# Moving the rotary update behind the fold and the normalisation in VectorE's order of a decoder's multi-query attention

## The reference

```
q = (x @ Wq + bq) in 16 heads;  k = x @ Wk + bk;  v = x @ Wv + bv
q, k = apply_rope(q), apply_rope(k)        # the first 4 of each head's 8 features are turned
att = softmax(causal(q @ k^T / sqrt(8)))
out = (att @ v in all heads) @ Wo + bo
x   = layernorm(x + out)
```

## Time and profile before

| what | value |
|---|---|
| three executions | 2307.48, 2312.87, 2314.32 us (median 2312.87) |
| the profiled execution's own time | 2307.48 us |
| its span | 2305.7 us |
| PE busy over the span | 1649.5 us (72%) |
| DVE busy | 1348.5 us (58%) |
| ACT busy | 915.9 us (40%) |
| POOL busy | 575.1 us (25%) |
| the stage of the change | from about 1548 to 1706 us of the span |
| length of one of its steps in the steady part | 9.12 to 9.21 us |

### The profile page before, as it was taken

How to read it: one execution, slowest core, us unless ns; L and a number is a source line. 1 busy time by engine, 2 the same in 40 slices (tenths; PEclk the granted TensorE clock), 3 DMA queues, 4 the chain that set the end, 5 groups by cost and what they waited for, 6 DMA issues and landing times.

```text
span 2305.7 us, 45150 instructions
## 1 busy us (share of the span) xinstructions
PE 1649.5 (72%) x14699; PEld 1055.1 (46%) x14699; DVE 1348.5 (58%) x4103; ACT 915.9 (40%) x2551; POOL 575.1 (25%) x965
## 2 busy tenths in 40 slices
PE   4443499477765565579777852138979999996998
PEld 3332355344433353445444521125547777774443
DVE  2333556466667756631675666756756666663776
ACT  2222444367531123224343433223336566563343
POOL 2321422111112222210122223431214434442010
PEclk9999999599977777789898975559999999997999
DMA  5000000000000000000002000000000000000000
GB/s 197 1 1 1 1 1 0 1 1 0 0 1 0 0 0 0 0 0 1 1 0 95 0 1 0 0 0 1 0 1 1 1 0 0 0 1 1 0 0 18
DMA packets 2926, 18.86 MB, mean 8 GB/s; under 512 B 1049, under 2 KB 1177, under 8 KB 1561
## 3 DMA queue, kind: packets, MB, share of 16 engines
q1 hardware_dynamic: 2842, 17.76, 2.1%
HBM read 16.64 MB, written 1.05 MB: 8 GB/s over the span
## 4 chain that ended last, share of the span: by engine, by line
PE 51%; issue 26%; DVE 7%; ACT 5%; POOL 5%; POOLq 4%; DVEq 2%; DMA 0%; ACTq 0%; SPq 0%
PE ps L2685 5%; PE ps L901 3%; PE ps L915 3%; PE ps L2250 3%; PE ps L2260 3%; PE ps L2274 3%; POOL arena L345 3%; PE ps L2229 3%; PE ps L2236 2%; PE ps L970 2%; PE ps L1438 2%; PE ps L2094 2%; PE ps L327 2%; PE ps L535 2%; PE ps L880 2%
## 5 line engine op out<-in xcount | busy, mean ns | idle before, releaser
L345 POOL TENSOR_TENSOR arena<-arena,C 128x1 f32<-128x1 f32 (+1 forms) x272 | 155.7, 574 | 810.8 <-DVE arena L356 499.0
L1060 DVE TENSOR_REDUCE arena<-ps 128x4 f32<-128x512 f32 x256 | 164.1, 686 | 90.1 <-PE ps L911 50.0
L2187 POOL TENSOR_TENSOR arena<-arena 128x512 f32<-128x512 f32 x128 | 132.7, 1042 | 234.3 <-DVE arena L2475 233.8
L436 POOL TENSOR_TENSOR arena<-arena,C 128x512 f32<-128x512 f32 x96 | 99.8, 1040 | 365.1 <-ACT arena L637 126.7
L1028 ACT ACTIVATE arena<-ps 128x512 f32<-128x512 f32 x256 | 132.2, 604 | 90.0 <-PE ps L927 90.0
L1438 PE MATMUL ps<-hid,WA 128*20 128x16 f32 x1024 | 57.3, 197 | 108.4 <-DVE hid L1481 108.4
L2685 PE MATMUL ps<-WA,arena 128*128 128x512 f32 x256 | 133.7, 604 | 0.4 <-ACT arena L2709 0.4
L2384 ACT ACTIVATE arena<-ps,arena 128x256 f32<-128x256 f32 x256 | 119.9, 478 | 11.9 <-issue 8.1
L2393 ACT COPY arena<-ps 128x512 f32<-128x512 f32 x128 | 69.1, 589 | 121.7 <-PE ps L2260 121.7
L1895 PE MATMUL ps<-C,arena 128*128 128x128 f32 x32 | 14.3, 469 | 133.2 <-ACT arena L1943 92.2
L2467 DVE TENSOR_REDUCE arena<-ps 128x2 f32<-128x512 f32 x128 | 82.5, 687 | 43.9 <-PE ps L2250 42.5
(11 more groups left out here) (412 smaller groups left out, 4204.6 us busy)
## 6 DMA issues: line engine op xcount, KB each, us to landing
WA<-w_late SPq DMA_DIRECT2D x1, 4228.0 KB, 13.6
R<-rows SPq DMA_DIRECT2D x1, 1858.0 KB, 8.4
WA<-w_early SPq DMA_DIRECT2D x1, 1600.0 KB
WB<-w_rest SPq DMA_DIRECT2D x1, 1152.0 KB, 12.9
xT_all<-x_T SPq DMA_DIRECT2D x1, 1024.0 KB, 6.8
x_all<-x_tok SPq DMA_DIRECT2D x1, 1024.0 KB, 15.2
arena<-mask SPq DMA_DIRECT2D x1, 1024.0 KB
ctxT_all<-ctx_T SPq DMA_DIRECT2D x1, 1024.0 KB
```

Of the source, the lines that this page charges most:

```text
L345: nc.gpsimd.tensor_tensor(v_(s, cols, "rstd", 0, n), v_(s, cols, "mv", 1, 2 * n - 1)[:, ::2] if n > 1 else v_(s, cols, "mv", 1, 1), cst("m ...
L436: return eng.tensor_tensor(heads(v_(s, ATT, dst, of, 512)), v_(s, ATT, src).unsqueeze(1).broadcast_to([128, 4, 128]), cst("tilemask").unsq ...
L1060: red = nc.vector.tensor_reduce(v_(z, ATT, "m", 4 * t, 4), heads(ps[z][t][:, :]), AXX, ALU.max)
L2187: nc.gpsimd.tensor_tensor(p, p, v_(z, LAT, "rec", 4 * u + 2 * x, 2).unsqueeze(2).broadcast_to([128, 2, 256]), ALU.mult).then_inc(l_sub, 1)
```

## The change

In VectorE's order of one step of `S_MQA`, the three instructions of `rope` for the next sequence move from ahead of the wait for `mT_ps` to behind the fold operand (line 1110) and `normed`, and stay ahead of `added`. Nothing is added or removed, and no other engine's order is touched.

```diff
@@ satt_dve, step @@
                 cut_up(s)
                 if before:
                     divided(i, s)
-                if sub == S_MQA and after:
-                    rope(i, s, 1)
                 dve.wait_ge(mT_ps, nth(st, i, s))
                 nc.vector.tensor_tensor(heads(v_(s, ATT, "P", FOLD, 256).bitcast(BF16)),
                                         ps[(s + 1) % 2][2][:, 0:128].unsqueeze(1).broadcast_to([128, 4, 128]),
@@
                                         ALU.mult).then_inc(m_fold, 1)
                 if before and not (isinstance(i, int) and 2 * i + s < 2):
                     normed(i, s, -2)
+                if sub == S_MQA and after:
+                    rope(i, s, 1)
                 if before:
                     added(i, s)
                 if after:
```

## The result

The changed kernel took 2342.31 us (median of four executions, 2341.67 to 2342.97), against 2313.35 us before (2307.48 to 2314.32). The ratio is 1.0129, with a 95% interval of 1.0113 to 1.0145: 29.0 us slower by the medians. The prediction was 2334 us with a range up to 2341, so the direction held and the size was above the range.

A forecast was written before the change was run, and what follows sets the result against it. PE was taken to bound the stage, its scores coming to wait for POOL's spreading. The 22.7 us sum gave 2330.2 us on the profiled time or 2335.6 on the median; predicted 2334 us, range 2326 to 2341.

The forecast's parts named there:

- The fold operand gained nothing: On DVE, L1110 waits for PE's L950, not the moved work, so it starts as before except in the first step.
- the slack of the spreading: Before the scores (L901), POOL's L436 had 0.87 us of usable slack; the rotary update moves 2.43 us later.
- `y_read` costs nothing further: L1086 starts at 1617.12 instead of 1616.46, but its `y_read` still comes before L436 ends at 1618.32.
- the sum: Delay of the scores (L901) over 15 steps: 19.8 + 1.3 + 1.6 = 22.7 us, with none made up.
- The clock.: In the changed stage, PE 79% busy with one 1.7 us gap per step was expected to keep clock 1.00.
- this rival: Granted clock falls in the changed stage: some 2460 us, or 2395 us if half the steps are hit; chance 3%.
- rows 1 and 9: Evidence against a fall: 1120 to 1220 us busy 75% at clock 0.99; LSTM stage busy 47% at 1.00.
- the 1.09 us from the start of L436 to that of L901: Term from POOL's spreading to PE's scores, taken from the first step, within the 3.29 us from L1110 to L901.

The follow-up runs named there:

- both repairs of PE's order: Changed kernel with seven extra matmuls per step in PE's gap and the wait for POOL's spreading last of the three before the scores: 2333.77 us.
- the gap filled with matmuls: Changed kernel with seven extra unread matmuls per step on PE between the fold and the scores: 2333.83 us.
- spreading twice: Kernel before, with POOL's spreading done twice in each step of the changed stage, VectorE's order untouched: 2318.58 us.
- only the sum moved: Against the kernel before, only the rotary update's sum moved behind the fold operand and `normed`, its two products staying ahead of the wait: 2323.77 us.
- the other order: Changed kernel with the rotary update directly behind the fold operand and the normalisation behind it: 2338.44 us.
- order of the waits: Changed kernel with the wait for POOL's spreading put last of the three in front of the scores, in the changed stage alone: 2338.45 us.
- spreading three times: Kernel before, with POOL's spreading done three times in each step of the changed stage, VectorE's order untouched: 2342.36 us.

## Why the prediction was right or wrong, step by step

**Right: the mechanism.** The fold operand gained nothing, the slack of the spreading was used up, the scores wait for POOL, `y_read` costs nothing further, and nothing behind the scores made the delay up. The size of the chain can be checked without the two effects that the sum lacked: with both repairs of PE's order the stage takes 157.95 us scores to scores against 134.99 before, 22.96 us more, where the sum said 22.7. By the medians of these two kernels it is 20.2 us.

**Wrong, the larger part: "The clock."** The prediction held the granted clock at 1.00, gave its fall 3% and had nothing for it in the sum. It fell in five steps, and the gap filled with matmuls shows what that cost: 167.61 - 159.92 = 7.7 us in the stage, 8.5 us by the medians. At the gap of 1.7 us that the prediction forecast itself it falls too. Neither row that was set against the fall carries the argument.

The earlier trace rows give the LSTM stage a clock of 1.00. The same stage of the kernel with the gap filled, which no edit touches, has 0.50 in that row, with matmuls of the same length: 194 ns in the median for L1438 (there L1443) and 388 ns for L1420 (there L1425). And behind that stage, in the kernel before, the same two matmuls take 0.73 us at 273.73 and 0.39 us at 288.49, while the clock row says 1.00 all the way. First the window of the kernel with the gap filled, then rows of the kernel before:

```profile
40.00:230.00 190.00, 88.71 (x1317) 60.00 (x1314) 60.65 (x349) 51.58 (x240) 48.01 (x100) 0.50 0.00 1
```

```profile
272.80:277.60 4.80, 4.58 (x20) 3.78 (x20) 0.00 (x0) 1.54 (x5) 1.80 (x4) 1.00 0.00 0
288.00:290.00 2.00, 2.00 (x17) 1.65 (x21) 1.05 (x5) 0.71 (x3) 0.25 (x1) 1.00 0.00 0
```

```profile
273.73 0.73 PE L880 MATMUL ps<-arena,WA 128*128 128x128 f32 x2
...
288.49 0.39 PE L880 MATMUL ps<-arena,WA 128*128 128x128 f32 x2
```

So the clock row of the kernel before can't be trusted up to about 277 us, and by the lengths of its matmuls the LSTM stage ran at the lower level. Its 110 waits of up to 1.5 us say nothing about gaps at the full clock. The stage at 1120 to 1220 us did run at the full clock, but from 1120 to 1213 us PE has no gap longer than 0.71 us.

The same trace held a case like the forecast one. From 836 to 882 us of the kernel before PE stands idle five times for 1.57 to 1.59 us, and behind three of these gaps the clock falls. The windows of that stage and one of the gaps:

```profile
836.00:882.00 46.00, 33.27 (x215) 26.65 (x213) 25.66 (x114) 18.38 (x68) 14.49 (x39) 0.89 0.00 0
852.00:857.00 5.00, 3.76 (x21) 3.27 (x22) 2.90 (x13) 2.20 (x9) 1.21 (x4) 0.79 0.00 0
```

```profile
853.08 0.33 PE L1780 MATMUL ps<-C,arena 128*128 128x128 f32 x1 [1.57 <-ACT arena L1810]
```

Nor does the longest gap alone decide. At the end of the first cross attention stage of the kernel before, PE is busy 73% with no gap longer than 0.71 us, and the clock falls:

```profile
406.00:414.00 8.00, 5.86 (x81) 2.68 (x73) 4.50 (x15) 3.37 (x7) 1.10 (x2) 1.00 0.01 2
414.00:416.00 2.00, 1.09 (x5) 0.60 (x5) 0.81 (x3) 0.13 (x1) 0.00 (x0) 0.65 0.00 0
```

Sorted by PE's idle time in front of the scores, the runs show in the changed stage: 0.18 to 0.26 us (before) no long step, 0.67 us (spreading twice) none, 1.27 (only the sum moved) none, 1.70 (the other order) three, 1.73 (order of the waits) four, 1.86 (spreading three times) four, 1.92 (the changed kernel) five. The price of this rival was mis-sized in the other direction: not all or half of the steps at half the clock (2395 to 2460 us), but five steps in which the lower level lasted a few microseconds, 1.3 to 1.6 us each against the same steps with the gap filled.

The Trainium skill, TensorE: Matmul & The Clock Gate, section "A second HAM failure mode: psum-queue depth-cycling", says that short idle times of PE between groups of matmuls can make the clock swing between its two levels. The prediction set it aside on rows 1 and 9; the traces of the changed kernel, of the spreading done three times and of the kernel before at 836 to 882 us agree with it; with gaps of up to 1.27 us in front of the scores the changed stage shows no such swing.

**Wrong, the smaller part: the 1.09 us from the start of L436 to that of L901.** It came from the first step, which stands ahead of the loop. In the loop it is 1.26 to 1.28 us. The edit of the wait order brought it back to 1.09 us, so what stands behind the wait on PE's queue is the cause. Why it costs something is argued and not shown: in the loop the following waits compare with values that depend on i, and the queue may get to them only when the first is met. By the two kernels with the gap filled the order is worth 1.97 us in the stage, about 0.18 us in each of the twelve steps of the loop less what the three others lost (0.02 to 0.10 us each).

**The sum, corrected.** 22.96 us (chain) + 1.97 us (waits) + 7.69 us (clock) = 32.62 us, the whole difference of the stage between the two profiled executions. The three terms are differences from one kernel to the next, so they add up by themselves; what the sum tests is its first term, 22.96 us against the forecast 22.7. The medians differ by 29.0 us. The executions behind the medians have no trace here, and scatter outside the changed stage, 2307.5 to 2314.3 us in the kernel before, is as large as what is missing, so the 3.6 us between the two stay unassigned.

**The prediction's own marks.** L1110 (now L1108) released by L950 with 1.65 to 1.76 us of idle time in most steps: as forecast. L901 released by L436: as forecast, with 1.9 instead of 1.7 us. Steps of 10.65 to 10.75 us: 10.85 us came. Clock below 0.95 in the stage was named as what would make the prediction wrong: it was 0.95 from 1568 to 1706 us.

## What to carry to other kernels

Where an engine's order is changed, ask for each wait of the bounding engine how much slack every one of its semaphores has, not only the one that ends it now: here the spreading had 0.7 us of slack, and the move took 2.4. When the sum leaves TensorE with a new gap, look through the whole trace for the places where the granted clock falls, at the gaps and the busy time ahead of them, and carry a second term for the clock if one of them resembles the new step; the mean clock and busy share of a long stretch can hide them. Before a clock row serves as evidence, compare the length of a matmul there with that of the same matmul elsewhere. A handover taken from an instruction ahead of a loop is not that of the loop: take the one with the same waits behind it.

## What the runs showed of the hardware that was not expected

Matmuls that nobody needs made a kernel faster: seven per step, 1.68 us of PE's time, took 8.5 us off the total by keeping the granted clock at 1.00. The fall of the clock came after the gap, not in it: ahead of all five long distances the 32 matmuls of the scores still ran at the full clock (1.17 us), and groups behind them at the lower. It also did not come in every step with the same gap, but in five of fifteen, three or four steps apart. The order of waits on one queue, all of which are met in the end, was worth about 0.18 us in each step of a loop. And a clock row of the profile said 1.00 over matmuls that took the time of the lower level.
